# A softmax-kernel attention and FP4 feed-forward block on one core, written anew, with one of three running sums on VectorE

## What is computed

```python
q = softmax(einsum(q, code) * scale) * scale
k_exp = exp(k - max(k, axis=tokens))
k_exp_cumsum = cumsum(k_exp, axis=tokens)
kv_cumsum = cumsum(einsum('bhtc,bhtd->bhtcd', k_exp, v), axis=tokens)
kv = kv_cumsum / (k_exp_cumsum[..., None] + 1e-09)
xo = einsum('bhtc,bhtcd->bhtd', q, kv)
...
gate, y = fp4_linear(xn, w_gate), fp4_linear(xn, w_up)
h = silu(gate) * y
return x + xo @ w_out.T + fp4_linear(h, w_down)
```

## Time and profile before

| | us |
|---|---|
| median of 3 runs | 136.61 (136.31 to 136.81) |
| span of the profiled execution | 134.5 |
| TensorE busy in it | 125.9 |
| VectorE busy | 121.8 |
| GpSimd busy | 116.5 |
| ScalarE busy | 114.0 |

### The profile page before, as it was taken

The page is one execution under the profiler, slowest core; times in us unless marked ns, Lnnn a source line. Parts: engine busy times, 40 slices in busy tenths (PEclk is TensorE's granted clock), DMA queues, the critical chain, the costliest instruction groups (busy, mean ns, idle before and its releaser), DMA issues.

```text
span 134.5 us, 2464 instructions
## 1 busy us (share of the span) xinstructions
PE 125.9 (94%) x821; PEld 106.4 (79%) x821; DVE 121.8 (91%) x293; ACT 114.0 (85%) x280; POOL 116.5 (87%) x118
## 2 busy tenths in 40 slices
PE   2999999795999999999999999999999998999992
PEld 2999977564577878887898798879887986889892
DVE  2789999898999899989998999899999997999971
ACT  0498997989999998999999999999998788698540
POOL 5387887899989999999999999999999999998600
DMA  4992000000000001000010002000200020010022
GB/s 110 276 389 88 5 2 0 2 0 2 0 0 5 0 0 77 1 0 5 35 43 0 2 5 80 0 0 0 78 5 0 0 78 0 0 58 25 0 97 59
DMA packets 4363, 5.14 MB, mean 38 GB/s; under 512 B 576, under 2 KB 2432, under 8 KB 4352
## 3 DMA queue, kind: packets, MB, share of 16 engines
q1 hardware_dynamic: 3264, 4.44, 9.5%
q10 hardware_dynamic: 1088, 0.56, 1.4%
...
## 4 chain that ended last, share of the span: by engine, by line
PE 78%; ACT 10%; DVE 4%; POOL 4%; issue 2%; POOLq 0%
PE at_ps L1910 5%; PE o_ps L2131 3%; PE o_ps L2115 3%; PE o_ps L1951 3%; PE o_ps L1842 2%; PE u_ps L2136 2%; ACT xn L653 2%; PE u_ps L1877 2%; PE u_ps L2021 2%; PE h_ps L2056 2%; PE h_ps L1901 2%; PE g_ps L2032 2%; PE g_ps L1890 2%; PE at_ps L1696 2%; PE at_ps L1719 2%; PE at_ps L1720 2%
## 5 line engine op out<-in xcount | busy, mean ns | idle before, releaser
L453 POOL TENSOR_TENSOR kv<-v_sb,kv 128x1024 f32<-128x1024 f32 x6 | 11.8, 1972 | 0.0
L361 POOL TENSOR_TENSOR o_codes<-kv,q_n 128x1024 f32<-128x1024 f32 x6 | 11.8, 1967 | 0.0
L1910 PEld LDWEIGHTS at_ps<-wqkv_t,xn_t 128*128 128x128 f32 x48 | 8.0, 190 | 3.2 <-DVE q_n L1285 2.2
L1910 PE MATMUL at_ps<-wqkv_t,xn_t 128*128 128x192 f32 x48 | 8.9, 328 | 1.6 <-DVE q_n L1285 1.6
L653 ACT ACTIVATE xn<-x_all,shift,rstd 128x128 f32<-128x128 f32 x24 | 9.8, 483 | 0.0
L402 POOL TENSOR_TENSOR yh<-h,h_r 128x704 f32<-128x704 f32 x6 | 8.3, 1388 | 1.2 <-ACT h_r L735 1.2
L344 POOL TENSOR_TENSOR hq<-qh,h_max 128x704 f32<-128x704 bf16 x6 | 8.3, 1385 | 0.1
L419 POOL TENSOR_TENSOR hq<-qh,h_max 128x704 f32<-128x704 bf16 x6 | 8.3, 1388 | 0.0
L483 POOL TENSOR_TENSOR yh<-h,h_r 128x704 f32<-128x704 f32 x6 | 8.3, 1391 | 0.0
L1099 DVE TENSOR_TENSOR kv<-kv,at_ps 128x1152 f32<-128x1152 f32 x6 | 8.0, 1337 | 0.0
L1044 ACT ACT_TABLE_LOAD x6 | 7.7, 1283 | 0.1
...
## 6 DMA issues: line engine op xcount, KB each, us to landing
...
```

The lines of the kernel that those rows point to most:

```text
L361: nc.gpsimd.tensor_tensor(o_codes[:, p, :, :].rearrange("p j (c w) -> p j c w", w=HEAD), kv[:, p, :, 0:KV].rearrange("p j (c w) -> p j c w ...
L453: nc.gpsimd.tensor_tensor(kv[:, p, :, 0:KV].rearrange("p j (c h w) -> p j c h w", c=CODE, w=HEAD), v_sb[:, p, :].rearrange("p (j h w) -> p ...
L1910: last = nc.tensor.matmul(at_ps[:, j // 2, j % 2 * QKV:(j % 2 + 1) * QKV], xn_t[:, p, j * P:(j + 1) * P], wqkv_t[:, :], start=(j % 2 == 0) ...
```

## The change

The program is written out anew, and all five queues have another order: no loop over steps, but one call after another, each with its batch, its tiles and its PSUM bank as arguments. The arithmetic of each stage stays. What is different, besides the order:

- The first of the three adds of each batch is on VectorE (its `add_tile`, called with j = 1); the second and third stay on GpSimd.
- The q exponentials, their sum and the guess of 1 / den stand in SBUF (q_exp, q_sum, den_exp) rather than in PSUM.
- The eight PSUM banks are one tensor `ps`, and each use names its bank. hq_t, den, silu and others have two buffers each.
- The layer norm's small steps (variance, square, ratio, root, shift) are on VectorE, for batches 1 to 7 with the guess by ln and exp; batch 0 keeps the power on GpSimd.
- Gate and up weights are handled one after the other, batch 0's x in two halves, and more h in single tiles. The last batch's hq products are on GpSimd.
- ScalarE has 13 table loads. The unread matmuls are 26.

```diff
+            def add_tile(b, j):
+                p = b % 2
+                return nc.vector.tensor_tensor(kv[:, p, j, :], kv[:, p, j, :], kv[:, p, j - 1, :], ALU.add)
...
+            def q_sum_of(b):
+                return nc.vector.tensor_reduce(q_sum[:, b % 2, :, :], q_exp[:, b % 2, :, :].rearrange("p j (c h) -> p j h c", c=CODE), AX.X, ALU.add)
...
+            def denominators(b):
+                p = b % 2
+                for c in range(CODE):
+                    last = nc.vector.scalar_tensor_tensor(out=den[:, p, :, c * HEADS:(c + 1) * HEADS], in0=kv[:, p, :, KV + c * HEADS:KV + (c + 1) * HEADS],
+                                                          scalar=DEN_EPS, in1=q_sum[:, p, :, :], op0=ALU.add, op1=ALU.mult)
+                return last
+
+            def den_check(b):
+                p = b % 2
+                return nc.vector.tensor_tensor(den_p[:, p, :, :], den_exp[:, p, :, :], den[:, p, :, :], ALU.mult)
+
+            def den_newton(b):
+                p = b % 2
+                return nc.vector.scalar_tensor_tensor(out=den_r[:, p, :, :], in0=den_p[:, p, :, :], scalar=2.0, in1=den_exp[:, p, :, :], op0=ALU.subtract, op1=ALU.mult)
+
+            def q_normal(b):
+                p = b % 2
+                return nc.vector.scalar_tensor_tensor(out=q_n[:, p, :, :], in0=q_exp[:, p, :, :], scalar=-HEAD_SCALE, in1=den_r[:, p, :, :], op0=ALU.mult, op1=ALU.mult)
...
+            def guess_square(lo, hi):
+                return nc.vector.scalar_tensor_tensor(out=guess_sq[:, lo:hi, :], in0=guess[:, lo:hi, :], scalar=-0.5, in1=guess[:, lo:hi, :], op0=ALU.mult, op1=ALU.mult)
+
+            def guess_ratio(lo, hi):
+                return nc.vector.tensor_tensor(ratio[:, lo:hi, :], guess_sq[:, lo:hi, :], var_eps[:, lo:hi, :], ALU.mult)
...
-                    nc.vector.tensor_reduce(a_ps[:, ROW + TILES * HC:ROW + TILES * (HC + HEADS)].rearrange("p (j h) -> p j h", j=TILES),
-                                            a_ps[:, ROW:ROW + TILES * HC].rearrange("p (j c h) -> p j h c", j=TILES, c=CODE), AX.X, ALU.add)
...
-                        last = nc.vector.scalar_tensor_tensor(out=den[:, :, c * HEADS:(c + 1) * HEADS], in0=kv[:, p, :, KV + c * HEADS:KV + (c + 1) * HEADS],
-                                                              scalar=DEN_EPS, in1=a_ps[:, ROW + TILES * HC:ROW + TILES * (HC + HEADS)].rearrange("p (j h) -> p j h", j=TILES),
-                                                              op0=ALU.add, op1=ALU.mult)
```

More of the change, by code:

```diff
@@ L330, in _ @@
+            sp.wait_ge(residt_done, 4)
+            sp.dma_start(out_v[7][:, 3*P:4*P], out_sb[:, 1, 3*P:4*P]).then_inc(last_stored, 16)
+            sp.wait_ge(stored[0], 64)
+            sp.wait_ge(stored[1], 48)
             sp.wait_ge(last_stored, 64)
@@ new lines, in unread, with qk_weights, w_transpose @@
+            def unread():
+                for _ in range(2):
+                    nc.tensor.matmul(ps[:, 7, 0:P], ident[:, :], before[:, :], start=True, stop=True)
+            def qk_weights(bank):
+                for s in range(2):
+                    last = nc.tensor.matmul(ps[:, bank, s * HC:(s + 1) * HC], wqk_raw[:, s, :], code_bd[:, s, :, :].rearrange("p c h -> p (c h)"), start=True, stop=True)
+                return last
+            def w_transpose(w, bank):
+                first = {"gate": 0, "up": FFP, "down": 2 * FFP}[w]
+                for c in range(CHUNKS):
+                    last = nc.tensor.transpose(ps[:, bank, c * P:(c + 1) * P], w_dq[:, first + c * P:first + (c + 1) * P], ident[:, :])
+                return last
@@ new lines, in transpose_xn, with qkv @@
+            def transpose_xn(b, bank):
+                for j in range(TILES):
+                    last = nc.tensor.transpose(ps[:, bank, j * P:(j + 1) * P], xn[:, b % 2, j * D:(j + 1) * D], ident[:, :])
+                return last
+            def qkv(b, bank):
+                for j in range(TILES):
+                    last = nc.tensor.matmul(ps[:, bank + j // 2, j % 2 * QKV:(j % 2 + 1) * QKV], xn_t[:, b % 2, j * P:(j + 1) * P], wqkv_t[:, :], start=(j % 2 == 0),
+                                            stop=False, skip_group_check=True)
+                return last
@@ new lines, in transpose_xq, with gate, up @@
+            def transpose_xq(b, lo, hi, bank):
+                for j in range(lo, hi):
+                    last = nc.tensor.transpose(ps[:, bank, j * P:(j + 1) * P], xq[:, b % 2, j * P:(j + 1) * P], ident[:, :])
+                return last
+            def gate(b, j, bank):
+                return nc.tensor.matmul(ps[:, bank, 0:FF], xq_t[:, b % 2, j * P:(j + 1) * P], w_t[:, 0:FF], start=True, stop=True)
+            def up(b, j, bank):
+                return nc.tensor.matmul(ps[:, bank, 0:FF], xq_t[:, b % 2, j * P:(j + 1) * P], w_t[:, FFP:FFP + FF], start=True, stop=True)
@@ new lines, in transpose_hq, with project @@
+            def transpose_hq(b, j, bank):
+                for c in range(CHUNKS):
+                    last = nc.tensor.transpose(ps[:, bank, c * P:(c + 1) * P], hq[:, b % 2, j, c * P:(c + 1) * P], ident[:, :])
+                return last
+            def project(b, bank, start):
+                for j in range(TILES):
+                    last = nc.tensor.matmul(ps[:, bank, j * P:(j + 1) * P], o_t[:, b % 2, j * P:(j + 1) * P], wo_t[:, :], start=(start and j == 0), stop=False, skip_group_check=True)
+                return last
```

3945 lines of the change are left out of this document (1965 added, 1980 removed).

## The result

The changed kernel takes **148.66 us** (148.15 to 149.07, 4 runs) beside 136.53 for the kernel before on the same chip: a ratio of 1.087, 95% interval 1.082 to 1.091. The prediction was 151.2, range 135.5 to 162. The mechanism it was built on is in the trace; several terms of the sum were mis-sized, in both directions.

What follows compares the result with a forecast made beforehand. VectorE was to become the bound in place of TensorE: 126.1 work + 2.8 and 2.1 at the ends + 16.1 waits + 2.0 idle = 149.1 us span; with 2.1 carried over to the median, 151.2 us, range 135.5 to 162.

Steps and rivals of the forecast that it cites:

- The deciding step: VectorE instructions with two SBUF inputs wait until GpSimd's running instruction is through: 16.1 us, between 0 and 28.6; chance 0.70.
- The rivals without a wait: Two SBUF inputs on VectorE cost nothing extra: 135.6 us (chance 0.14), 136.0 to 137.2 (0.05) or 140.9 (0.11).
- The whole sum: VectorE's span: 126.1 work, 2.8 before and 2.1 behind, 16.1 waits, 2.0 idle between, 149.1 us.
- The agreement of 16.1: Predicted VectorE waits behind GpSimd: 46 of 61 two-SBUF-input instructions charged 0.35 us each, 16.1 us.
- The two thirds: Mean wait cut from at most 0.54 to 0.35 us, as records also cover issue and write-back, when no input is read.
- VectorE's sum without waits: VectorE busy time: 121.8, plus 2.9 adds, less 1.7 hq products, plus 2.0 layer norm, plus 1.1 halves: 126.1 us.
- The first rival: No wait and a tighter queue: VectorE bound, idle between falls from 7.8 to 2.5, time 135.6 us; chance 0.14.
- My sum for TensorE: TensorE's end: first gate matmul at 21.7, about 104.5 us of work left, plus 2.4: 128.6 us.
- Start: First gate matmul comes later, at 21.7 us (21 to 23) against 17.20, gate weights being dequantised at about 19.5.
- Clock: Danger named: TensorE, idle more often, is granted a clock below 1.00, its matmuls lengthen and it could be bound again.
- Busy for about three quarters: TensorE, waiting for VectorE, was to be busy for about three quarters of the span.
- The add: Moving the first add to VectorE makes GpSimd's second add wait; costed at nothing, or 0.44 us a batch were VectorE ahead.

Runs made afterwards that it cites:

- m1_cost: Stand-alone kernel of VectorE loops, most beside a GpSimd loop: a spaced 128-wide instruction with two SBUF inputs took 284 ns beside idle GpSimd, 612 beside products.
- a4_reduce: Changed kernel with the 40 normaliser instructions made one-input reductions of the same width (attention comes out wrong): 138.33 us.
- a5_no_lock: Changed kernel with normaliser, eight adds and 13 small layer-norm instructions all made reductions, so none has two SBUF inputs (results wrong): 131.52 us.
- b1_norm_sbuf: Kernel before with only the normaliser's q_exp, q_sum and den_exp moved from PSUM to SBUF tiles: 158.14 us.
- b2_add_vectore: Kernel before with only the first of the three adds moved from GpSimd to VectorE in batches 1 to 6: 138.50 us.
- l1_ln_pairs: Changed kernel, nothing left out, with only the layer norm's 13 two-input instructions rewritten as reductions over pairs: 146.66 us.
- a2_add_gpsimd: Changed kernel with the first of the three adds put back on GpSimd in all eight batches: 149.21 us.
- The loops above: Stand-alone kernels of VectorE loops beside GpSimd loops; those in step with GpSimd had waits of 0.33, 0.51 and 0.91 us beside instructions of 1.39, 0.80 and 1.97.

## Why the prediction came out as it did

**The deciding step held.** Two SBUF inputs on VectorE wait behind a GpSimd instruction that reads SBUF. It is shown three ways: by the cost itself (m1_cost), by taking it away (a4_reduce, a5_no_lock) and by putting it into the kernel before (b1_norm_sbuf, b2_add_vectore). Without the waits the changed kernel would be 17.1 us faster, by busy time 16.5 (137.5 - 121.0), against 16.1 in the sum. The rivals without a wait are excluded by the rows of the groups.

**The whole sum.** By the profiled execution the span is 2.8 + 2.1 before and behind VectorE's data, 121.0 of work, 16.5 of waits and 4.0 idle between: 146.4. The prediction had 126.1, 16.1 and 2.0: 149.1. So a work term 5.1 too high was partly made up by an idle term 2.0 too low, and only the waits came out as said.

**The agreement of 16.1 is partly luck.** Per group, records against a5_no_lock, the waits are: den 16 x 0.36 = 5.7, den_p 3.2, q_n 1.8, add 1.9, den_r 1.4, the 13 small ones 3.9, in all 17.9, or 0.29 for each of the 61. The sum charged 40 normaliser and add instructions and 6 small ones at 0.35 each: 14.0 and 2.1. The two thirds by which it came from 0.54 to 0.35 rested on no row. It left the second den out, which waits like the first (b1_norm_sbuf), and took the same price for all, where den_p pays 0.39 and den_r 0.18. The small ones paid 3.9, not 2.1; they stand in the start, where I had half of them hidden.

**VectorE's sum without waits: 126.1 said, 121.0 measured.** The records of all groups add up to 139.5 before and 143.5 in a5_no_lock, 4.0 more, which looks like the 4.3 of the sum. But the sum counted steps, which leave the overlap of neighbouring records out, and records hold it. What overlaps (records less busy time) is 17.7 us over 293 instructions before and 22.5 over 326 in a5_no_lock, 0.060 and 0.069 each. As an estimate from these figures, 33 more instructions at the old overlap make the added work 2.0 of busy time, not 4.3, and the closer queue takes off another 2.8; so both the added steps and adding them to a busy time of before were wrong. The idle time between fell as well, from 7.8 to about 3.5 us (4.0 in the changed kernel), where I had 2.0.

**The first rival had the right sign on its own ground.** "No wait, and a tighter queue" had 135.6 with VectorE as the bound; without waits it was 131.5, with TensorE on 90% of the chain. My sum for TensorE, 128.6, was the one to take: the span was 129.5. The new order was worth more than I gave it.

**Start.** First gate matmul at 21 to 23 predicted, 24.3 measured; without waits it is 21.5, my 21.7. The missing 2.8 us come back when neither the small instructions nor the adds wait (a5_no_lock). With both still waiting and the normaliser freed it is 25.1 (a4_reduce); with the small ones alone rewritten, 23.0 (l1_ln_pairs). So at least 1.3 us are theirs, and the rest isn't parted. The sum had put these waits on VectorE's account but not into the start's.

```profile
L1857 PE MATMUL ps<-w_t,xq_t x64: 459/459/563, 24.3 to 114.9; 128*128 128x352 f32 x64
```

**Clock.** I had named a granted clock below 1.00 as a danger. It came, once: in the changed kernel's profile TensorE stood for 3.89 us before 19.73, waiting for VectorE's k_max (5.59 of the 10 us from 10 to 20 are busy), and from 20 to 23 us its granted clock was 0.50, the lower of its two levels, 1.2 GHz; over 20 to 30 that makes 0.84. It cost nothing that VectorE did not cover: the runs of l1_ln_pairs at either clock agree, and a4_reduce, with 0.83 in that stretch, is 10 us faster than the changed kernel.

**TensorE and GpSimd.** "Busy for about three quarters" was wrong for TensorE: 87%. Its work was to be that of before, 125.9 us, and 125.9 of 149 is 84%, as I could have worked out. GpSimd's 78% is near the 75% said, with 114.3 us against 111.4. Without waits it is 112.9, so 1.5 of the 2.9 were missing from the sum and 1.4 came with the waits: the adds take 814 ns instead of 800 (a5_no_lock), yx 1101 instead of 1062, as the wait is mutual (m1_cost).

**The add.** I held that its move is free for GpSimd's queue because VectorE is late. GpSimd did wait for it, 4.1 us in all; it had the room. What I did not see is that taking the add away would give nothing back (a2_add_gpsimd): the waits of a batch are no fixed price per instruction. The add's own mean moves too, from 664 ns to 818 in a4_reduce, where the normaliser no longer waits. Why they pass from one instruction to the next stays open: GpSimd's higher share, 82% for 78, was to give 0.7 us of more waiting, and it was 4.9. The loops above suggest that the place at which VectorE meets GpSimd's queue decides; that is not shown in the kernel.
